# Cross-attention on one core: the last 65 keys' value products stacked into 128 rows

## What is computed

```python
q = einsum('bsd,ed->bse', layernorm(x), Wq)
k = einsum('btd,ed->bte', ctx, Wk)
v = einsum('btd,ed->bte', ctx, Wv)
attn = softmax(einsum('bse,bte->bst', q, k) * 256 ** -0.5)
x = x + einsum('bst,bte->bse', attn, v)
```

## Time and profile before

| | us |
|---|---|
| median of 3 runs | 405.71 |
| the runs | 403.99, 406.04, 405.71 |
| the profiled execution | 403.98 |
| its span, first to last instruction | 402.1 |
| PE busy in the span | 391.7 |
| VectorE, ScalarE, GpSimd busy | 299.0, 228.8, 215.8 |

### The profile page before, as it was taken

The page is one execution under the profiler, slowest core; times in us unless marked ns, Lnnn a source line. Parts: engine busy times, 40 slices in busy tenths (PEclk is TensorE's granted clock), DMA queues, the critical chain, the costliest instruction groups (busy, mean ns, idle before and its releaser), DMA issues.

```text
span 402.1 us, 7798 instructions
## 1 busy us (share of the span) xinstructions
PE 391.7 (97%) x2584; PEld 363.4 (90%) x2584; DVE 299.0 (74%) x1093; ACT 228.8 (57%) x516; POOL 215.8 (54%) x209
## 2 busy tenths in 40 slices
PE   6999999999999999999999999999999999999877
PEld 6888888899999999999999999999878998999766
DVE  4798677886766957576674857653786899999996
ACT  3886849454765465454654533352556657678462
POOL 1688999774376323254420210010147767999993
PEclk9999999999999999999999999999999999999999
DMA  8900213003433313224111000000100000000101
GB/s 232 306 3 1 80 56 96 17 0 114 119 125 97 100 48 84 58 58 129 49 44 51 0 2 2 1 2 0 28 2 2 0 2 0 29 29 27 41 28 65
DMA packets 19992, 21.36 MB, mean 53 GB/s; under 512 B 3181, under 2 KB 16625, under 8 KB 19953
## 3 DMA queue, kind: packets, MB, share of 16 engines
q1 hardware_dynamic: 18832, 19.96, 16.6%
q10 hardware_dynamic: 1120, 0.92, 0.9%
HBM read 18.78 MB, written 2.10 MB: 52 GB/s over the span
## 4 chain that ended last, share of the span: by engine, by line
PE 80%; POOL 11%; DVE 4%; issue 3%; DMA 1%; ACT 0%; SPq 0%; DVEq 0%; ACTq 0%; POOLq 0%
PE keep_pQ L76 11%; PE keep_pQ L77 11%; PE keep_pQ L78 11%; POOL ffn_prod L1259 9%; PE context_pA L1052 6%; PE context_pA L1054 6%; PE context_pA L1053 6%; PE context_pR L1086 6%; PE context_pR L534 3%; PE context_pA L534 3%; POOL ffn_near L1327 2%; PE context_pR L76 2%; PE context_pR L78 2%; PE context_pR L77 2%; PE ffn_pK L1812 2%
## 5 line engine op out<-in xcount | busy, mean ns | idle before, releaser
L900 DVE TENSOR_TENSOR att_pTl<-context_pR,att_pTh 128x512 fp32r<-128x512 f32 x64 | 37.0, 587 | 29.7 <-ACT att_pTh L812 29.4
L1259 POOL TENSOR_TENSOR ffn_prod<-ffn_first,ffn_near 128x1024 f32<-128x1024 f32 (+1 forms) x29 | 54.1, 1884 | 2.0 <-DVE ffn_first L1689 2.0
L812 ACT ACTIVATE att_pTh<-context_pR 128x512 fp32r<-128x512 f32 x64 | 32.1, 515 | 40.0 <-PE context_pR L1086 40.0
L931 DVE TENSOR_REDUCE att_mx<-keep_pQ 128x1 f32<-128x402 f32 x64 | 34.7, 565 | 8.2 <-PE keep_pQ L78 7.8
L852 ACT ACTIVATE att_prob<-keep_pQ,att_nmax 128x1206 f32<-128x1206 f32 x16 | 20.3, 1269 | 35.9 <-DVE att_nmax L936 35.8
L787 POOL TENSOR_TENSOR keep_rstd<-att_ve,keep_mhalf 128x4 f32<-128x4 f32 x3 | 3.0, 1007 | 56.5 <-DVE att_ve L990 56.5
L1842 PE MATMUL ffn_pT<-keep_ident,ffn_prod 128*128 128x128 f32 x240 | 28.8, 273 | 4.1 <-POOL ffn_prod L1259 4.1
L1842 PEld LDWEIGHTS ffn_pT<-keep_ident,ffn_prod 128*128 128x128 f32 x240 | 26.8, 141 | 6.4 <-DVE ffn_hT L1722 4.6
L1086 PE MATMUL context_pR<-keep_ident,att_prob 128*128 128x128 f32 (+1 forms) x208 | 31.8, 272 | 0.2 <-DVE att_pTl L900 0.2
L1052 PE MATMUL context_pA<-att_pTh,att_cNh 128*128 128x256 f32 (+1 forms) x104 | 30.9, 297 | 0.0
L1052 PE MATMUL context_pA<-att_pTh,context_cNh 128*128 128x256 f32 (+1 forms) x104 | 30.9, 297 | 0.0
(11 more groups left out here) (337 smaller groups left out, 1285.0 us busy)
## 6 DMA issues: line engine op xcount, KB each, us to landing
keep_raw<-in_ctxT SPq DMA_DIRECT2D x24, 256.0 KB, 2.7
keep_raw<-in_ctx SPq DMA_DIRECT2D x24, 256.0 KB, 3.1
out<-keep_x SPq DMA_DIRECT2D x16, 128.0 KB, 1.7
keep_x<-in_x SPq DMA_DIRECT2D x3, 512.0 KB, 10.3
gru_wout<-in_W_out SPq DMA_DIRECT2D x1, 512.0 KB, 8.4
keep_raw<-in_fWq SPq DMA_DIRECT2D x2, 256.0 KB
keep_raw<-in_ctxT SPq DMA_DIRECT2D x8, 32.5 KB, 3.0
keep_raw<-in_ctx SPq DMA_DIRECT2D x4, 65.0 KB
```

The costliest lines, as they stand in the source:

```text
L812: act.activation(to, bank, ACT.Copy).then_inc(bank_high, 1)
L900: dve.tensor_tensor(to, bank, half(it, 0, n)[0].bitcast(F32), ALU.subtract).then_inc(bank_free, 1)
L931: last = dve.tensor_reduce(mx[:, h, j:j + 1], pS[:, j, 0:min(SPANS[j][1], CTX) - SPANS[j][0]], AX.X, ALU.max)
L1259: return eng.tensor_tensor(prod[:, i % PB, a:b].rearrange("p h (i j) -> p h i j", j=KEYS), (factor if factor is not None else first[:, n % ...
```

## The change

In place of three products of 65 rows each over the last key tile, two products of 128 rows are made. The sum ph.ch + ph.cl + pl.ch over keys 0 to 64 of that tile is laid out in rows:

- first product: rows 0 to 64 pair the high halves of both sides; row 65 pairs the high half of key 64's probability with the low half of its context row; row 96 pairs the low half of its probability with the high half of its context row; the context's rows 66 to 95 and 97 to 127 are zero.
- second product: rows 0 to 63 pair the high half of p with the low half of c, rows 64 to 127 the low half of p with the high half of c, for keys 0 to 63.

What each engine does for it:

- **Loads**: the last piece of each batch is four DMAs in place of one, all on SyncE's queue and all on the buffer's semaphore (64 rows of 1 KB written twice beside each other; the same 64 rows once more, to partitions 64 to 127; the last key to partitions 64 and 65; the last key to partition 96). ScalarE waits for all four (`arrived`).
- **ScalarE, per last piece**: four copies in place of one: 66 rows of 256 with a scale per row taken from a column of the identity (zero but for row 65), 1 row of 256, 128 rows of 256, then, after a wait for the first of them, 65 rows of 256 in place in the raw buffer.
- **GpSimd, per last piece**: two subtractions (66 and 64 rows of 256) in place of one of 65. Once per buffer set, a memset of 128 x 256 of the last key tile: in the recurrence's opening, between the memsets of line 211 and the first product of line 235, and after the recurrence, behind the memsets of line 792.
- **ScalarE, per query tile**: one more exponential, without a sum: the last key's score, read again and again, into 63 more columns of `prob`. The second increment of `exp_ready` moves to it.
- **TensorE**: P3 transposes 128 columns in place of 65; A3 and B3 are two matmuls in place of three.
- **P3's eviction**: ScalarE writes the bank of 128 x 128 twice beside each other (`pLast`, 128 x 256) in place of 65 x 128; VectorE does two subtractions in place of one: bank rows 0 to 63 into rows 64 to 127 of the second copy, and rows 96 to 127 of the first copy.

The columns 65 to 127 of P3 are the last key's probability again, which is what rows 65 and 96 of the first product need.

```diff
+LONE, TAIL_LOADS = 96, 4
...
+def load_tail(eng, src, raw, loaded):
+    n, both = CLAST - 1, raw.rearrange("p (m d) -> p m d", d=D)
+    eng.dma_start(both[0:n], src[0:n].unsqueeze(1).broadcast_to([n, 2, D])).then_inc(loaded, 16)
+    eng.dma_start(both[n:2 * n, 1], src[0:n]).then_inc(loaded, 16)
+    eng.dma_start(both[n:n + 2, 0], src[n:n + 1].broadcast_to([2, D])).then_inc(loaded, 16)
+    eng.dma_start(both[LONE:LONE + 1, 0], src[n:n + 1]).then_inc(loaded, 16)
+
+def tail_high(act, raw, keys, mixed, ident, tail_read, count):
+    n = CLAST
+    act.activation(keys[0:n + 1], raw[0:n + 1, 0:D], ACT.Copy, scale=ident[0:n + 1, n:n + 1])\
+        .then_inc(tail_read, 1)
+    act.activation(keys[LONE:LONE + 1], raw[LONE:LONE + 1, 0:D], ACT.Copy)
+    act.activation(mixed, raw[:, D:2 * D], ACT.Copy)
+    act.wait_ge(tail_read, count)
+    return act.activation(raw[0:n, 0:D].bitcast(F32R), raw[0:n, 0:D], ACT.Copy)
+
+def tail_low(pool, raw, keys, mixed):
+    a, e = CLAST - 1, CLAST + 1
+    pool.tensor_tensor(keys[0:e], raw[0:e, 0:D], keys[0:e].bitcast(F32), ALU.subtract)
+    return pool.tensor_tensor(mixed[0:a], raw[0:a, D:2 * D], mixed[0:a].bitcast(F32), ALU.subtract)
...
-        pool.wait_ge(pad_set, 2)
+        pool.memset(keep["cNh"][0][:, CT - 1].bitcast(F32), 0.0).then_inc(pad_set, 1)
+        pool.wait_ge(pad_set, 3)
...
                     act.activation(prob[:, g % 2, full:CTX], pS[:, KB - 1, 0:CTX - full], ACT.Exp,
                                    bias=nmax[:, g % 2:g % 2 + 1], scale=ATT_SCALE,
-                                   accum_out=part[:, g % 2, 1:2]).then_inc(exp_ready, 1)
+                                   accum_out=part[:, g % 2, 1:2])
+                    act.activation(prob[:, g % 2, CTX:], pS[:, KB - 1, CTX - 1 - full:CTX - full]
+                                   .broadcast_to([P, CT * P - CTX]), ACT.Exp, bias=nmax[:, g % 2:g % 2 + 1],
+                                   scale=ATT_SCALE).then_inc(exp_ready, 1)
...
+            if it[0] == "P" and it[2] == NG - 1:
+                bank, (keys, mixed) = pR[:, n % RING, 0:P], (half(it, 0, n)[0][:, m] for m in range(2))
+                dve.tensor_tensor(mixed[CLAST - 1:P], bank[0:CLAST - 1], keys[0:CLAST - 1].bitcast(F32), ALU.subtract)
+                dve.tensor_tensor(keys[LONE:P], bank[LONE:P], keys[LONE:P].bitcast(F32), ALU.subtract)\
+                    .then_inc(bank_free, 1)
+                return
...
+                    if kt == CT - 1:
+                        pe.matmul(out, l[0], pLast[:, 0], start=False, stop=False)
+                        last = pe.matmul(out, l[1], pLast[:, 1], start=False, stop=True)
+                        continue
+                    r = [t[:, kt] for t in pT]
                     pe.matmul(out, l[0], r[0], start=(kt == 0), stop=False)
                     pe.matmul(out, l[0], r[1], start=False, stop=False)
-                    last = pe.matmul(out, l[1], r[0], start=False, stop=(kt == CT - 1))
+                    last = pe.matmul(out, l[1], r[0], start=False, stop=False)
```

More of the change, by code:

```diff
@@ L65, in context_pieces, with is_tail, arrived @@
                     lambda s: raw[:, s].rearrange("p (t d) -> p t d", d=D), ch[par][:, t:t + 2], cl[par][:, t:t + 2]))
-    out.append((d["ctx"][b, (CT - 1) * P:CTX, :], lambda s: raw[0:CLAST, s, 0:D],
-                ch[par][0:CLAST, CT - 1], cl[par][0:CLAST, CT - 1]))
-    return out
+    out.append((d["ctx"][b, (CT - 1) * P:CTX, :], lambda s: raw[:, s], ch[par][:, CT - 1], cl[par][:, CT - 1]))
+    return out
+def load_tail(eng, src, raw, loaded):
[16 more added lines that the diff above has]
+    return pool.tensor_tensor(mixed[0:a], raw[0:a, D:2 * D], mixed[0:a].bitcast(F32), ALU.subtract)
+def is_tail(i):
+    return i % PIECES == PIECES - 1
+def arrived(i):
+    return sum(16 * (TAIL_LOADS if is_tail(j) else 1) for j in range(i % RAW, i + 1, RAW))
 def split_products(pe, out, pairs):
@@ L303, in scalar @@
                 for i in pieces_at(n):
-                    act.wait_ge(ld_piece[i % RAW], 16 * (i // RAW + 1))
-                    _, raw, hi, _ = pieces[i]
+                    act.wait_ge(ld_piece[i % RAW], arrived(i))
+                    _, raw, hi, lo = pieces[i]
+                    if is_tail(i):
+                        act.wait_ge(pad_set, 3)
+                        tail_high(act, raw(i % RAW), hi, lo, ident, tail_read, 1).then_inc(piece_hi, 1)
+                        continue
                     act.activation(hi, raw(i % RAW), ACT.Copy).then_inc(piece_hi, 1)
@@ L683, in stage_attention @@
     qT = (qT0, qT1)
-    pT = [st.sb(n, [P, CT, 2 * P], F32R) for n in ("pTh", "pTl")]
+    pT = [st.sb(n, [P, CT - 1, 2 * P], F32R) for n in ("pTh", "pTl")]
+    pLast = st.sb("pLast", [P, 2, 2 * P], F32R)
     vT = [st.sb(n, [P, DC, 2 * P], F32R) for n in ("vTh", "vTl")]
@@ L741, in half @@
             return qT[a % 2][which][:, i], bank
+        if kind == "P" and i == NG - 1:
+            return pLast[:, :, a % 2 * P:(a % 2 + 1) * P], bank[:, 0:P].unsqueeze(1).broadcast_to([P, 2, P])
         if kind == "P":
-            rows = CLAST if GROUPS[i][-1] == CT - 1 else P
             m = len(GROUPS[i])
-            return pT[which][0:rows, GROUPS[i][0]:GROUPS[i][0] + m, a % 2 * P:(a % 2 + 1) * P], \
-                bank[0:rows, 0:m * P].rearrange("p (t n) -> p t n", n=P)
+            return pT[which][:, GROUPS[i][0]:GROUPS[i][0] + m, a % 2 * P:(a % 2 + 1) * P], \
+                bank[:, 0:m * P].rearrange("p (t n) -> p t n", n=P)
     def wait_overwrite(eng, it):
@@ L763, in sync @@
                 sp.wait_ge(piece_lo, n - RAW + 1)
+            if is_tail(n):
+                load_tail(sp, src, raw(n % RAW), ld_piece[n % RAW])
+                continue
             sp.dma_start(raw(n % RAW), src).then_inc(ld_piece[n % RAW], 16)
@@ L792, in gpsimd @@
             pool.memset(m[:, :, CTX:CPAD].bitcast(F32), 0.0).then_inc(pad_set, 1)
+        pool.memset(cNh[1][:, CT - 1].bitcast(F32), 0.0).then_inc(pad_set, 1)
         for g in range(TILES):
@@ L821, in piece_high @@
         def piece_high(i):
-            act.wait_ge(ld_piece[i % RAW], 16 * (i // RAW + 1))
+            act.wait_ge(ld_piece[i % RAW], arrived(i))
             wait_context(act, i)
-            _, raw, hi, _ = pieces[i]
+            _, raw, hi, lo = pieces[i]
+            if is_tail(i):
+                act.wait_ge(pad_set, 3)
+                tail_high(act, raw(i % RAW), hi, lo, ident, gru["tail_read"], i // PIECES + 2).then_inc(piece_hi, 1)
+                return
             act.activation(hi, raw(i % RAW), ACT.Copy).then_inc(piece_hi, 1)
@@ L1084, in item @@
                 for m, kt in enumerate(GROUPS[i]):
-                    rows = CLAST if kt == CT - 1 else P
-                    last = pe.transpose(bank[0:rows, m * P:(m + 1) * P], prob[:, a % 2, kt * P:kt * P + rows],
-                                        ident[:])
+                    last = pe.transpose(bank[:, m * P:(m + 1) * P], prob[:, a % 2, kt * P:(kt + 1) * P], ident[:])
             else:
```

20 lines of the change are left out of this document (15 added, 5 removed).

## The result

The changed kernel takes 406.15 us in the median of 22 runs, the kernel before 404.09 us in 22 runs beside it: a ratio of 1.0034, interval 1.0021 to 1.0048. It is slower by 0.2 to 0.5%, or 1.4 us, where I had forecast 0.9 us less than before. The number given, 404.8 us, hung on the median of three runs, 405.71; over more runs the kernel before has 404.1, so the range (403.0 to 406.3) holds the time, and the sign is wrong all the same. A second series on another chip gave 405.19 us in 12 runs against 404.33 in 35: 1.0023, interval 1.0002 to 1.0044.

A forecast was written before the change was run, and what follows sets the result against it. TensorE, busy throughout the attention stage, was taken to bound the kernel: -1.9 us for removed matmuls plus 1.0 us wait in slot 3 gives -0.9, so 404.8 us from 405.71, range 403.0 to 406.3.

The forecast's parts named there:

- The saving: Attention, last key tile: 16 of 48 matmuls removed at 0.12 us each, coming through whole, -1.9 us.
- The evictions of P3 and the exponential: Every tile: P3's bank free 0.5 us later, within 0.86 us of cover in tight even slots; cost nothing, 0.36 left.
- slower: P3's eviction: Rival: new eviction over 0.86 us longer, TensorE waits in four tight even slots; 407.4 us at 1.5 longer; chance 0.09.
- It does not do what it says: Rival: two matmuls of 128 rows keep the distance of three, 0.18 us each; 406.7 us; chance 0.02.
- The last piece in slot 3: Four DMAs and copies delay ScalarE's exponential; TensorE waits 1.0 us for P0's bank at P3's transpose (0.3 to 2.3).
- Free: Rival: slot 3's DMAs land early or slack was miscounted, all 1.9 us stay; 403.8 us; chance 0.22.
- break-even through long ends: Rival: long ends of issue, landing and copies in slot 3, wait 1.9 to 2.3; 405.7 to 406.1 us; chance 0.14.
- The memset: GpSimd in the recurrence's opening: about 0.4 us for 128 x 256, taken up by a 0.97 us wait at 22.51; cost nothing.
- 128 rows or 65, the distance stays: Products over the last key tile: matmuls of 128 and 65 rows lie between 276 and 283 ns, so rows cost nothing.
- The rival on the other side: The slower rival: P3's longer eviction makes TensorE wait in the four tight even slots; 407.4 us; chance 0.09.
- The start of the sum: Forecast counted from 405.71 us, the median of three runs of the kernel before, down 0.9 to 404.8.

The follow-up runs named there:

- loads alone: Change's four loads, copies, subtractions and memsets, with the kernel before's P3, evictions, three products and tile places; 405.22 us, 1.0021 to the kernel before.
- the variant with 0.96 busy: Kernel before plus one memset of 128 x 1024, four times the change's, in GpSimd's opening; 405.84 us, 1.0029.
- The places alone: Kernel before, same computation and three products, with tiles sized as in the change so that several lie elsewhere; 405.46 us against 404.58, 1.0025.
- the loads undone: Changed kernel with one load, one copy and one subtraction per last piece, and two memsets in the opening; 404.41 us, 1.0000 to the kernel before.
- the run with a product less: Kernel before with the third product of the last key tile (low half of its context rows) left out; 403.09 us, 0.9952.

## Why the prediction was wrong

By its own steps:

- **The saving.** Right in mechanism, a little less in size: -1.7 by the trace and -1.8 by the medians, for -1.9.
- **The evictions of P3 and the exponential.** Right: 0.5 us later, 0.34 left for 0.36, no wait. The rival "slower: P3's eviction" is out. "It does not do what it says" is out too.
- **The last piece in slot 3.** Right in place, instruction and size: a wait of 0.92 for 1.0; loads alone cost 0.93 of the attention's length, and taking them out of the change gave 1.28. That the wait came so near is in part luck. Its parts erred in both directions and cancelled: issue 1.81 for 1.3, copies 1.59 for 1.4, landing 1.30 for 2.05. "Free" and "break-even through long ends" are out.
- **The memset: the step that failed by reasoning.** "A wait of 0.97 at 22.51 takes it up": I took an idle stretch for slack. The wait ends with VectorE's work, and that hangs, one step further back, on the very products that the memset delays. It took 0.31 busy and 0.25 on the path, where the sum had nothing, and the variant with 0.96 busy cost 0.8.
- **The places: the step that was missing.** "128 rows or 65, the distance stays" was right, and I took it that with this the other products kept theirs. The sizes of the tiles, which the diff shows, got no price. Batches 0 and 2 hold 4 pairs of query tiles with 2 x 38 or 2 x 39 products each, of which some 250 have such a neighbour, and 250 x 2.4 ns = 0.6 us. The places alone cost 0.65 of the attention's length (1.2 at full clock). Restoring them gave 0.58 back, though the wait in slot 3 was 0.2 longer there (1.1 for 0.9), and 0.8 at full clock (+0.82 and +0.03 against the kernel before in either batch).
- **The rival on the other side** had its place in the evictions. Neither it nor the forecast had a cost outside the new instructions, and there the loss was.

- **The start of the sum.** 405.71, the median of three runs, was 1.6 us above that of 22 (404.09). That the time lies inside the range owes much to this: -0.9 us from 404.1 would have been 403.2, 3 us below the measured median.

The sum becomes -1.7 (saving) + 0.9 (slot 3) + 0.65 (places) = -0.1 us in the attention, each term from a run of its own, where the trace has +0.09; with 0.25 for the memset it is +0.15, against +0.34. The span of that execution is 0.5 longer, but its opening began 0.43 earlier and held the longer scan, 0.55, that the memset does not cause. The medians at full clock have +0.8 (404.43 against 403.61, three runs of the one). The first series' +0.34% is 1.4 us; its six runs at full clock lie 0.7 us above the median of all 22 runs of the kernel before. So the runs account for the sign, narrowly, and for 0.15 to 0.35 us of the size; what is left up to 0.8 at full clock and 1.4 over all runs stays open. Part of it may be that 24 of 33 runs of the changed kernel had a mean clock below 0.9975, against 16 and 21 of 35 of the kernel before in the first two batches; in the third it was 22 of 35 for the kernel before, so this may as well be chance.

## What to carry to other kernels

A wait behind an added instruction hides it only if what ends the wait doesn't itself depend on that instruction: follow the releaser back one more step before you call an idle stretch slack. Where TensorE is busy all the time, compare the distance of unchanged matmuls before and after: a tile that changes its size moves all behind it, and here that cost some 0.6 us of the 1.7 that 16 removed matmuls brought. A last piece that is loaded in parts goes where nothing waits behind it; this change pays (0.9965 and 0.9971) only once its loads and its memset stand elsewhere.

## What the runs showed of the hardware

- **The distance of matmuls goes by the operands' places.** 128 x 256 products in a row: 117.0 or 119.4 ns, by some 500 bytes between the two operands' tiles. The Trainium skill, page "SBUF — State Buffer", section "Operand start alignment", asks for starts at a multiple of the element's size and says of itself that it is "about legality, not speed". All starts here are multiples of 32 bytes, and the speeds differ; which distances are bad, beyond the four tried, no run shows.
- **How long a load holds its queue goes neither by its bytes nor by its rows alone.** In slot 3 the load of 64 rows of 1 KB written twice kept SyncE for 0.63 us, that of the same rows once into partitions 64 to 127 for 0.61, that of one row into two partitions for 0.44, and that of one row for 0.25. The plain load of 65 rows kept it for 0.34 in the kernel before and with the loads undone. What makes the difference, no run shows. ScalarE had all four 1.30 us after the last one's issue began.
- **A copy of one row is no cheaper than one of 128.** ScalarE: 1x256 took 0.41 us, 128x256 0.42, and 66x256 with a scale per row 0.51.
- **The granted clock falls for a few microseconds in some executions**, of every kernel, with the one before as well. Stretches of the run with a product less, in the feed-forward part (us, busy us and instructions of PE, PEld, DVE, ACT, POOL, clock, DMA):

```profile
320.85:324.27 3.42, 3.42 (x30) 3.28 (x28) 3.38 (x32) 2.73 (x10) 3.02 (x3) 1.00 0.00 0
324.27:327.68 3.41, 3.41 (x22) 3.41 (x22) 1.95 (x20) 1.03 (x5) 1.12 (x1) 0.62 0.03 7
327.68:331.09 3.41, 3.41 (x18) 3.41 (x18) 3.11 (x24) 1.16 (x6) 2.62 (x2) 0.50 0.00 0
```

  The clock goes from its upper level to 0.50, 1.2 GHz, and is back behind 331.5 us, while TensorE counts as busy in all of it and in the stretch before. What it ran from 321.5 us on are products of 4 and of 128 columns:

```profile
321.51 1.84 PE L1813 MATMUL ffn_pK<-ffn_group_of,ffn_sq 128*128 128x4 f32 x16
323.21 1.14 PE L1822 MATMUL keep_pQ<-ffn_keyT,ffn_qT 128*128 128x128 f32 x8
324.19 2.59 PE L1813 MATMUL ffn_pK<-ffn_group_of,ffn_sq 128*128 128x4 f32 x16
326.64 2.05 PE L1822 MATMUL keep_pQ<-ffn_keyT,ffn_qT 128*128 128x128 f32 x8
```

  The second group of either kind, which took 1.84 and 1.14 us at the upper level, takes 2.59 (the clock falls within it) and 2.05. The kernel before runs the same products, and in its profile the clock stays at 1.00. Such an execution is 1 to 2.5 us longer: the kernel before has medians of 403.77, 404.64 and 405.88 us at mean clocks of 1.00, about 0.996 and about 0.992 (second batch of runs). That is as much as the whole effect of this change, so the executions must be compared clock by clock.
